# Ternary network: second products of even and odd tiles in two PSUM banks, the last two tiles in gate banks with scales of their own, and the last store in halves

## The chip, the cores and the metric

One core of a Trainium2 chip runs one program. The metric is the device time of that program in microseconds; three runs of the kernel before are shown.

## The reference

The program is a stack of four layers on x of shape 4 x 512 x 16 x 16 in f32 (1024 tokens of 512 channels): an attention layer, a mixture of experts, a scan over image rows, and last a feed-forward network with ternary weights. Only the last one is touched:

```python
    xn = _rmsnorm(x)                    # inside _bitlinear(x, w)
    scale = 127.0 / clip(max(abs(xn)), EPS);  xq = clip(round(xn * scale), -32, 127) / scale
    wq = clip(round(w / mean(abs(w))), -1, 1) * mean(abs(w))
    ...
    gate = silu(_bitlinear(x, w1))      # 512 -> 1408
    up = _bitlinear(x, w2)              # 512 -> 1408
    return _bitlinear(gate * up, w3)    # 1408 -> 512, then t = t + this
```

So h = gate * up needs its own mean square and its own maximum per token before it can be rounded and multiplied with w3. The maximum and the mean square run over all 1408 columns of a token.

## The kernel before

`ternary_ffn` is the last stage, from about 885 us on. The tokens stand in NT = 8 tiles of 128 (tile t is the tokens t * 128 and on). Each engine has a program of its own, written out by hand in the order in which it runs; semaphores with a running count tie them together. Per tile t:

- TensorE multiplies the rounded input `q_cm` with w1 and w2 in three parts (512, 512 and 384 columns). Part g = 3t + i goes to the gate banks `gu_ps[2 * (g % 2)]` (g0 or g1) and `gu_ps[2 * (g % 2) + 1]` (u0 or u1).
- ScalarE takes silu of the gate, VectorE multiplies by the other half into `h` (`h_ready`, a count of parts).
- VectorE takes the maximum (`h_max`), ScalarE the sum of squares (`square`, `hsq_ready`).
- VectorE works out the scales of a pair of tiles in a chain of small steps, each of which waits for the one before (`rsqrt`, `quant_scale`, L81 to L87 and L1920 to L1924; `hscale_ready`).
- ScalarE multiplies and rounds (`h_round`), VectorE clips to bf16 (`h_quant`, tile `hq`), TensorE transposes it into the banks `ht` (`turn_h`), ScalarE copies it to `h_cm` (`h_copy`).
- TensorE multiplies with w3 into the bank `y_ps` (`second`, 11 matmuls), VectorE adds to the tokens `x_tm` (`add_y`, `x4_ready`), TensorE transposes back into the bank `x_ps` (`turn_out`), ScalarE copies to `out_cm` (`out_copy`, `out_ready`), and SyncE stores one image (two tiles, 512 KB) at a time.

All eight PSUM banks are in use: g0, u0, g1, u1, two `ht`, `x_ps` and `y3_ps`. The pair (t - 3, t - 2) is finished while tile t (odd) is under way; the last pair, 6 and 7, comes after the loop. `second(t)` waits for `x4_ready` at t, because all tiles share `y_ps`; `turn_out(t)` waits for `out_ready` at t, because all share `x_ps`.

Of the kernel before, what the change touches and what calls it, by code (L numbers as in the profile page):

```python
# [1627 lines left out]
def ternary_ffn(nc, io, keep):  # L1628
# [7 lines left out]
    with ctx:  # L1636
# [72 lines left out]

        def col(i, t):  # L1710
            return stat[:, i, t:t + 1]
# [7 lines left out]

        def scale_and_round(eng, engine, t, done):  # L1720
            eng.wait_ge(q_scale_ready, t // HALF_TILES + 1)
            engine.tensor_scalar(z[:, t, :], z[:, t, :], col(Q, t), ROUND, ALU.mult, ALU.add).then_inc(done, 1)

        @block.sync
        def _(sp):
            for n in range(BATCH):
                sp.wait_ge(out_ready, 2 * n + 2)
                sp.dma_start(io["out"][n].rearrange("(k p) h w -> p k (h w)", p=P),
                             out_cm[:, :, n * SP:(n + 1) * SP]).then_inc(out_sent, 16)
            sp.wait_ge(out_sent, 16 * BATCH)  # L1730
# [11 lines left out]
        def _(act):  # L1742
# [24 lines left out]
            def h_round(t):  # L1767
                act.wait_ge(hscale_ready, t // 2 + 1)
                S.activation(h[:, t % 4, :], h[:, t % 4, :], ACT.Copy, bias=ROUND, scale=col(HQ, t)).then_inc(hr_ready, 1)
# [8 lines left out]
            def out_copy(t):  # L1778
                act.wait_ge(x4_turned, t + 1)
                S.copy(out_cm[:, :, t * P:(t + 1) * P], x_ps[:, :].rearrange("p (k m) -> p k m", k=KC)).then_inc(out_ready, 1)  # L1780
# [3 lines left out]
            for t in range(NT):  # L1784
                for i, (c, n) in enumerate(PARTS):
                    g = 3 * t + i
                    act.wait_ge(gu_summed, g + 1)
                    if g >= 2:
                        act.wait_ge(h_ready, g - 1)
                    S.activation(silu[:, g % 2, 0:n], gu_ps[2 * (g % 2)][:, 0:n], ACT.Silu,  # L1790
                                 scale=col(G_SCALE, t)).then_inc(silu_ready, 1)

                    if t % 2 == 0 and t >= 2 and i < 2:
                        h_round(t - 2 + i)
                    if t % 2 and t >= 3 and i == 0:
                        h_copy(t - 3)
                    if t % 2 and i == 1:
                        square(t - 1)
                for j in TURN_AFTER.get(t, ()):
                    q_copy(j)  # L1800
                if t >= 4 and t % 2 == 0:
                    out_copy(t - 4)
                if t % 2:
                    if t >= 3:
                        h_copy(t - 2)
                    square(t)
                    if t >= 5:
                        out_copy(t - 4)
            h_round(NT - 2)
            h_round(NT - 1)  # L1810
            out_copy(NT - 4)
            h_copy(NT - 2)
            out_copy(NT - 3)
            h_copy(NT - 1)
# [4 lines left out]
        def _(pe):  # L1819
# [30 lines left out]
            def second(t):  # L1850
                pe.wait_ge(h_cm_ready, 2 * t + 2)
                if t:
                    pe.wait_ge(x4_ready, t)
                else:
                    pe.wait_ge(x3_ready, NT)
                for k in range(W3):
                    mm = T.matmul(y_ps[:, :], h_cm[:, t % 2, k, :], w3[:, k, :], start=(k == 0), stop=(k == W3 - 1))  # L1857
                mm.then_inc(y_summed, 1)

            def turn_out(t):  # L1860
                pe.wait_ge(x4_ready, t + 1)
                if t:
                    pe.wait_ge(out_ready, t)
                for k in range(KC):
                    mm = T.transpose(x_ps[:, k * P:(k + 1) * P], x_tm[:, t, k * P:(k + 1) * P], ident[:, :])  # L1865
# [4 lines left out]
            for t in range(NT):  # L1870
# [14 lines left out]
                if t >= 4 and t % 2 == 0:  # L1885
                    turn_out(t - 4)
                if t % 2 and t >= 3:
                    turn_h(t - 2)
                    second(t - 3)
                    if t >= 5:  # L1890
                        turn_out(t - 4)
                    second(t - 2)
            turn_out(NT - 4)
            turn_h(NT - 2)
            turn_out(NT - 3)
            second(NT - 2)
            turn_h(NT - 1)
            second(NT - 1)
# [4 lines left out]
        def _(dve):  # L1903
# [56 lines left out]
            def add_y(t):  # L1960
                dve.wait_ge(y_summed, t + 1)
                V.scalar_tensor_tensor(x_tm[:, t, :], y_ps[:, :], col(Y_SCALE, t), x_tm[:, t, :],
# [25 lines left out]
            for t in range(NT):  # L1988
                for i, (c, n) in enumerate(PARTS):
                    g = 3 * t + i  # L1990
                    dve.wait_ge(silu_ready, g + 1)
                    V.scalar_tensor_tensor(h[:, t % 4, c:c + n], gu_ps[2 * (g % 2) + 1][:, 0:n], col(U_SCALE, t),  # L1992
                                           silu[:, g % 2, 0:n], ALU.mult, ALU.mult).then_inc(h_ready, 1)
# [6 lines left out]
                if t % 2:  # L2000
# [3 lines left out]
                    dve.wait_ge(dve_step, done[0])  # L2004
                    dve.wait_ge(hsq_ready, t + 1)
                    rsqrt(nc, link, cols(HRMS, t - 1, t + 1), cols(HSS, t - 1, t + 1), 1.0 / W1, RMS_EPS, scratch)
                    quant_scale(t - 1, t + 1, HRMS, HMAX, HA, HQ, Y_SCALE).then_inc(hscale_ready, 1)
                    link(V.tensor_scalar(cols(Y_SCALE, t - 1, t + 1), cols(Y_SCALE, t - 1, t + 1), inv_ws[:, 2:3], None, ALU.mult))
                    if t >= 3:
                        add_y(t - 2)  # L2010
            for t in (NT - 2, NT - 1):
                h_quant(t)
            for t in (NT - 2, NT - 1):
                add_y(t)
# [48 lines left out]
```

## Time and profile before

| | |
|---|---|
| median of 3 runs | 1003.87 us (999.87 to 1004.82) |
| profiled execution | 999.2 us, span 997.6 us |
| TensorE busy in the span | 929.6 us (93%) |
| VectorE, ScalarE busy | 634.0 us (64%), 543.4 us (54%) |
| mean granted clock of TensorE | 0.972 |

Positions in the text are microseconds from the span's start. The profiled time is that of the whole execution, the span what the profiler saw of it, first to last instruction or transfer. In the trace `h` is written at L1992, its maximum is L1952, `h_round` L1769, `square` L1765, `h_quant` L1958, `h_copy` L1775 and L1776, `second` L1857, `add_y` L1962, `turn_out` L1865, `out_copy` L1780 and the store L1728.

### The profile page before, as it was taken

How to read it: one execution, taken by the hardware profiler on the slowest of the kernel's cores; microseconds unless marked ns; L12 is line 12 of the kernel's file. 1: busy time of each engine (PE TensorE's matmuls, PEld its weight loads, DVE VectorE, ACT ScalarE, POOL GpSimd, SP SyncE). 2: the span in 40 equal slices, each digit the busy share in tenths (PEclk: the TensorE clock that was granted, in tenths of full speed). 3: DMA queues.
4: the chain of work that ended last, by engine and by line, in shares of the span. 5: the costliest groups of instructions: out<-in, count | busy, mean ns of one | idle time of the engine just before them, and what ended most of it. 6: DMA issues, size and time to landing. Idle time of an engine off the chain costs nothing. (4 is left out here: it accounts for less than half of the span.)

```text
span 997.6 us, 20461 instructions
## 1 busy us (share of the span) xinstructions
PE 929.6 (93%) x7568; PEld 612.2 (61%) x7569; DVE 634.0 (64%) x1281; ACT 543.4 (54%) x857; POOL 149.1 (15%) x174
## 2 busy tenths in 40 slices
PE   5998996999999999999999999999999979967795
PEld 4545543677766666766677677668764448743452
DVE  5388695557754645755656655665666876677673
ACT  3685776456654544655556655655653213235674
POOL 0000101001220120120120122012106720002000
PEclk9999998999999999999999999999999979987999
DMA  8770646678776567676578857857796610000001
GB/s 289 269 246 2 250 158 193 212 216 269 249 254 219 181 221 221 220 262 211 185 239 253 280 202 236 269 179 252 257 274 217 182 31 3 4 2 1 1 22 64
DMA packets 165038, 181.93 MB, mean 182 GB/s; under 512 B 54753, under 2 KB 132577, under 8 KB 164994
## 3 DMA queue, kind: packets, MB, share of 16 engines
q1 hardware_dynamic: 152354, 147.35, 45.8%
q0 software_dynamic: 9936, 32.12, 9.7%
q10 hardware_dynamic: 2704, 1.87, 0.6%
q8 instruction: 28, 0.46, 0.2%
q14 instruction: 16, 0.13, 0.0%
HBM read 155.09 MB, written 14.68 MB: 170 GB/s over the span
## 5 line engine op out<-in xcount | busy, mean ns | idle before, releaser
L1094 DVE SCALAR_TENSOR_TENSOR w_lo<-raw_first,w_hi 128x1024 f16<-128x1024 f32 x144 | 172.6, 1219 | 53.4 <-ACT w_hi L585 53.4
L852 PE MATMUL pa<-x,w_hi 128*128 128x256 f16 (+2 forms) x576 | 171.3, 297 | 2.9 <-DMA x<-early 2.5
L853 PE MATMUL pa<-x,w_hi 128*128 128x256 f16 (+2 forms) x576 | 171.3, 297 | 0.0
L854 PE MATMUL pa<-x,w_lo 128*128 128x256 f16 (+2 forms) x576 | 171.3, 297 | 0.0
L852 PE MATMUL pb<-x,w_hi 128*128 128x256 f16 (+2 forms) x576 | 170.6, 296 | 0.0
L853 PE MATMUL pb<-x,w_hi 128*128 128x256 f16 (+2 forms) x576 | 170.6, 296 | 0.0
L854 PE MATMUL pb<-x,w_lo 128*128 128x256 f16 (+2 forms) x576 | 170.6, 296 | 0.0
L1101 DVE SCALAR_TENSOR_TENSOR between<-pb,between 128x320 f32<-128x320 f32 (+1 forms) x144 | 73.8, 513 | 132.5 <-ACT between L589 132.4
L585 ACT ACTIVATE w_hi<-raw_first 128x1024 f16<-128x1024 f32 x144 | 147.8, 1050 | 15.3 <-PE pt L854 12.9
L1094 DVE SCALAR_TENSOR_TENSOR w_lo<-raw_last,w_hi 128x1024 f16<-128x1024 f32 x72 | 87.7, 1217 | 57.2 <-ACT w_hi L585 57.2
L593 ACT CAST early<-between 128x320 f16<-128x320 f32 (+1 forms) x144 | 68.4, 475 | 94.6 <-DVE between L1101 94.6
L585 ACT ACTIVATE w_hi<-raw_last 128x1024 f16<-128x1024 f32 x72 | 75.9, 1054 | 63.3 <-PE pe_ L926 27.2
L589 ACT ACTIVATE between<-pa 128x320 f32<-128x320 f32 (+1 forms) x144 | 65.3, 454 | 78.1 <-PE pb L854 77.5
L1106 DVE TENSOR_TENSOR early<-between,early 128x320 f16<-128x320 f32 (+1 forms) x144 | 73.1, 508 | 10.7 <-ACT early L593 10.5
L459 POOL DMA_DIRECT2D slot_y<-chunks x16 | 12.3, 767 | 416.5 <-ACT chunks L601 416.5
L852 PEld LDWEIGHTS pa<-x,w_hi 128*128 128x128 f16 x576 | 56.6, 98 | 25.0 <-issue 3.5
L854 PEld LDWEIGHTS pa<-x,w_lo 128*128 128x128 f16 x576 | 56.6, 98 | 20.4
L853 PEld LDWEIGHTS pa<-x,w_hi 128*128 128x128 f16 x576 | 56.5, 98 | 20.3
L852 PEld LDWEIGHTS pb<-x,w_hi 128*128 128x128 f16 x576 | 56.5, 98 | 20.0
L854 PEld LDWEIGHTS pb<-x,w_lo 128*128 128x128 f16 x576 | 56.4, 98 | 20.1
L853 PEld LDWEIGHTS pb<-x,w_hi 128*128 128x128 f16 x576 | 56.4, 98 | 19.9
L443 POOL DMA_INDIRECT early<-tokens,slot_ids x48 | 60.7, 1264 | 22.5 <-POOL slot_ids L451 12.8
(283 smaller groups left out, 1608.9 us busy)
## 6 DMA issues: line engine op xcount, KB each, us to landing
raw_first<-in_gate_up SPq DMA_DIRECT2D x96, 512.0 KB, 4.7
raw_last<-in_gate_up SPq DMA_DIRECT2D x32, 512.0 KB, 3.7
raw_first<-in_down SPq DMA_DIRECT2D x32, 512.0 KB, 5.0
raw_last<-in_down SPq DMA_DIRECT2D x32, 512.0 KB, 3.6
chunks<-in_f SPq DMA_DIRECT2D x16, 704.0 KB, 5.5
slot_y<-chunks POOLq DMA_DIRECT2D x16, 512.0 KB, 3.3
chunks<-in_f SPq DMA_DIRECT2D x6, 768.0 KB, 4.7
raw_first<-in_sgate SPq DMA_DIRECT2D x6, 512.0 KB, 6.0
```

Source lines behind the costliest of these rows:

```text
L443: pool.indirect_dma_start(out=rows16[0:w, j, :], out_offset=None, in_=io["tokens"], in_offset=bass.IndirectOffsetOnAxis(ap=ids[0:w, j:j + ...
L459: pool.dma_start(io["slot_y"][bass.ds(base_slot, 2 * P), :].rearrange("(j p) c -> p j c", p=P), y_sb[:, 0:2, :]).then_inc(y_out, 16)
L585: S.mul(w_hi[:, j % RING, c], raw[j % RING][:, c], W_SCALE).then_inc(hi_ready, 1)
L589: S.activation(gated[:, m % 2, 0:n], gate_ps[m % 2][:, 0:n], ACT.Silu, scale=1.0 / W_SCALE).then_inc(silu_ready, 1)
L593: S.copy(h_hi[:, m, 0:n], hid[:, m % 2, 0:n]).then_inc(h_hi_ready, 1)
L852: T.matmul(out, hi_a, hi_b, start=first, stop=False, **flags)
L853: T.matmul(out, hi_a, lo_b, start=False, stop=False, **flags)
L854: return T.matmul(out, lo_a, hi_b, start=False, stop=last, **flags)
L1094: V.scalar_tensor_tensor(w_lo[:, j % RING, c], raw[j % RING][:, c], W_SCALE, w_hi[:, j % RING, c], ALU.mult, ALU.subtract).then_inc(split_ ...
L1101: V.scalar_tensor_tensor(hid[:, m % 2, 0:n], up_ps[m % 2][:, 0:n], 1.0 / W_SCALE, gated[:, m % 2, 0:n], ALU.mult, ALU.mult).then_inc(hid_r ...
L1106: V.tensor_tensor(h_lo[:, m, 0:n], hid[:, m % 2, 0:n], h_hi[:, m, 0:n], ALU.subtract).then_inc(h_ready, 1)
```

## The change

Tiles share two banks in turn: `turn_ps(t)` is `x_ps` for even and `y_ps` for odd tiles, and both the second product of tile t and its transpose back use it. For tiles 6 and 7 the second product goes to g0 and g1, which the gates have left by then. `second(t)` waits for the output copy of tile t - 2 in place of the add of tile t - 1. Both transposes back of a pair and both output copies stand after the even tile's parts. For tile 7 the order is written out: tile 6 and tile 7 each get scales of their own (`SCALED` is the count of `hscale_ready` that a tile waits for), tile 6 is rounded, transposed and multiplied before tile 7's scales are ready, and the adds of tiles 4 and 5 come after tile 7's scales. The last image is stored in two halves, one for each tile. The other layers are unchanged.

```diff
@@ -1709,2 +1709,4 @@
+        SCALED = [1, 1, 2, 2, 3, 3, 4, 5]
+
         def col(i, t):
@@ -1719,2 +1721,8 @@
+        def turn_ps(t):
+            return (x_ps, y_ps)[t % 2]
+
+        def sum_ps(t):
+            return turn_ps(t) if t < NT - 2 else gu_ps[2 * (t - NT + 2)]
+
         def scale_and_round(eng, engine, t, done):
@@ -1725,3 +1733,3 @@
         def _(sp):
-            for n in range(BATCH):
+            for n in range(BATCH - 1):
                 sp.wait_ge(out_ready, 2 * n + 2)
@@ -1729,3 +1737,7 @@
                              out_cm[:, :, n * SP:(n + 1) * SP]).then_inc(out_sent, 16)
-            sp.wait_ge(out_sent, 16 * BATCH)
+            for t in range(NT - 2, NT):
+                sp.wait_ge(out_ready, t + 1)
+                sp.dma_start(io["out"][BATCH - 1].rearrange("(k p) h w -> p k (h w)", p=P)[:, :, t % 2 * P:(t % 2 + 1) * P],
+                             out_cm[:, :, t * P:(t + 1) * P]).then_inc(out_sent, 16)
+            sp.wait_ge(out_sent, 16 * (BATCH + 1))
@@ -1767,3 +1779,3 @@
             def h_round(t):
-                act.wait_ge(hscale_ready, t // 2 + 1)
+                act.wait_ge(hscale_ready, SCALED[t])
                 S.activation(h[:, t % 4, :], h[:, t % 4, :], ACT.Copy, bias=ROUND, scale=col(HQ, t)).then_inc(hr_ready, 1)
@@ -1779,3 +1791,3 @@
                 act.wait_ge(x4_turned, t + 1)
-                S.copy(out_cm[:, :, t * P:(t + 1) * P], x_ps[:, :].rearrange("p (k m) -> p k m", k=KC)).then_inc(out_ready, 1)
+                S.copy(out_cm[:, :, t * P:(t + 1) * P], turn_ps(t)[:, :].rearrange("p (k m) -> p k m", k=KC)).then_inc(out_ready, 1)
@@ -1794,5 +1806,7 @@
                         h_round(t - 2 + i)
+                    if t == NT - 1 and i == 0:
+                        square(t - 1)
                     if t % 2 and t >= 3 and i == 0:
                         h_copy(t - 3)
-                    if t % 2 and i == 1:
+                    if t % 2 and t < NT - 1 and i == 1:
                         square(t - 1)
@@ -1802,2 +1816,3 @@
                     out_copy(t - 4)
+                    out_copy(t - 3)
                 if t % 2:
@@ -1805,11 +1820,10 @@
                         h_copy(t - 2)
+                    if t == NT - 1:
+                        h_round(t - 1)
                     square(t)
-                    if t >= 5:
-                        out_copy(t - 4)
-            h_round(NT - 2)
+            h_copy(NT - 2)
             h_round(NT - 1)
+            h_copy(NT - 1)
             out_copy(NT - 4)
-            h_copy(NT - 2)
             out_copy(NT - 3)
-            h_copy(NT - 1)
             out_copy(NT - 2)
@@ -1851,8 +1865,10 @@
                 pe.wait_ge(h_cm_ready, 2 * t + 2)
-                if t:
-                    pe.wait_ge(x4_ready, t)
-                else:
+                if t < 2:
                     pe.wait_ge(x3_ready, NT)
+                elif t < NT - 2:
+                    pe.wait_ge(out_ready, t - 1)
+                else:
+                    pe.wait_ge(h_ready, 3 * (NT - 1) + t - NT + 4)
                 for k in range(W3):
-                    mm = T.matmul(y_ps[:, :], h_cm[:, t % 2, k, :], w3[:, k, :], start=(k == 0), stop=(k == W3 - 1))
+                    mm = T.matmul(sum_ps(t)[:, :], h_cm[:, t % 2, k, :], w3[:, k, :], start=(k == 0), stop=(k == W3 - 1))
                 mm.then_inc(y_summed, 1)
@@ -1861,6 +1877,6 @@
                 pe.wait_ge(x4_ready, t + 1)
-                if t:
-                    pe.wait_ge(out_ready, t)
+                if t >= NT - 2:
+                    pe.wait_ge(out_ready, t - 1)
                 for k in range(KC):
-                    mm = T.transpose(x_ps[:, k * P:(k + 1) * P], x_tm[:, t, k * P:(k + 1) * P], ident[:, :])
+                    mm = T.transpose(turn_ps(t)[:, k * P:(k + 1) * P], x_tm[:, t, k * P:(k + 1) * P], ident[:, :])
                 mm.then_inc(x4_turned, 1)
@@ -1886,2 +1902,3 @@
                     turn_out(t - 4)
+                    turn_out(t - 3)
                 if t % 2 and t >= 3:
@@ -1889,10 +1906,8 @@
                     second(t - 3)
-                    if t >= 5:
-                        turn_out(t - 4)
                     second(t - 2)
-            turn_out(NT - 4)
             turn_h(NT - 2)
-            turn_out(NT - 3)
             second(NT - 2)
             turn_h(NT - 1)
+            turn_out(NT - 4)
+            turn_out(NT - 3)
             second(NT - 1)
@@ -1961,3 +1976,3 @@
                 dve.wait_ge(y_summed, t + 1)
-                V.scalar_tensor_tensor(x_tm[:, t, :], y_ps[:, :], col(Y_SCALE, t), x_tm[:, t, :],
+                V.scalar_tensor_tensor(x_tm[:, t, :], sum_ps(t)[:, :], col(Y_SCALE, t), x_tm[:, t, :],
                                        ALU.mult, ALU.add).then_inc(x4_ready, 1)
@@ -1987,8 +2002,18 @@
             dve.wait_ge(dve_step, done[0])
-            for t in range(NT):
-                for i, (c, n) in enumerate(PARTS):
-                    g = 3 * t + i
-                    dve.wait_ge(silu_ready, g + 1)
-                    V.scalar_tensor_tensor(h[:, t % 4, c:c + n], gu_ps[2 * (g % 2) + 1][:, 0:n], col(U_SCALE, t),
-                                           silu[:, g % 2, 0:n], ALU.mult, ALU.mult).then_inc(h_ready, 1)
+            def gated(t, i):
+                g, (c, n) = 3 * t + i, PARTS[i]
+                dve.wait_ge(silu_ready, g + 1)
+                V.scalar_tensor_tensor(h[:, t % 4, c:c + n], gu_ps[2 * (g % 2) + 1][:, 0:n], col(U_SCALE, t),
+                                       silu[:, g % 2, 0:n], ALU.mult, ALU.mult).then_inc(h_ready, 1)
+
+            def h_scales(t0, t1):
+                dve.wait_ge(dve_step, done[0])
+                dve.wait_ge(hsq_ready, t1)
+                rsqrt(nc, link, cols(HRMS, t0, t1), cols(HSS, t0, t1), 1.0 / W1, RMS_EPS, scratch)
+                quant_scale(t0, t1, HRMS, HMAX, HA, HQ, Y_SCALE).then_inc(hscale_ready, 1)
+                link(V.tensor_scalar(cols(Y_SCALE, t0, t1), cols(Y_SCALE, t0, t1), inv_ws[:, 2:3], None, ALU.mult))
+
+            for t in range(NT - 1):
+                for i in range(len(PARTS)):
+                    gated(t, i)
                     if t % 2 == 0 and t >= 2 and i >= 1:
@@ -2003,13 +2028,20 @@
                         add_y(t - 3)
-                    dve.wait_ge(dve_step, done[0])
-                    dve.wait_ge(hsq_ready, t + 1)
-                    rsqrt(nc, link, cols(HRMS, t - 1, t + 1), cols(HSS, t - 1, t + 1), 1.0 / W1, RMS_EPS, scratch)
-                    quant_scale(t - 1, t + 1, HRMS, HMAX, HA, HQ, Y_SCALE).then_inc(hscale_ready, 1)
-                    link(V.tensor_scalar(cols(Y_SCALE, t - 1, t + 1), cols(Y_SCALE, t - 1, t + 1), inv_ws[:, 2:3], None, ALU.mult))
+                    h_scales(t - 1, t + 1)
                     if t >= 3:
                         add_y(t - 2)
-            for t in (NT - 2, NT - 1):
-                h_quant(t)
-            for t in (NT - 2, NT - 1):
-                add_y(t)
+
+            t = NT - 1
+            h_max(t - 1)
+            gated(t, 0)
+            h_scales(t - 1, t)
+            gated(t, 1)
+            gated(t, 2)
+            h_max(t)
+            h_quant(t - 1)
+            h_scales(t, t + 1)
+            add_y(t - 3)
+            add_y(t - 2)
+            h_quant(t)
+            add_y(t - 1)
+            add_y(t)
```

**TensorE, tiles 2 and 3 being finished** (at the end of tile 5; `ht` is the transposed h, `y_ps` and `x_ps` the two banks, `g` a gate bank). Before:

```order
L1847 MATMUL ht<-ident_b,hq 128x128 [waits h_cm_ready,hq_ready]
L1847 MATMUL ht<-ident_b,hq 128x128 x10
L1857 MATMUL y_ps<-ternary,h_cm 128x512 [waits x4_ready,h_cm_ready]
L1857 MATMUL y_ps<-ternary,h_cm 128x512 x10
L1865 MATMUL x_ps<-ident,x_tm 128x128 [waits out_ready,x4_ready]
L1865 MATMUL x_ps<-ident,x_tm 128x128 x3
L1857 MATMUL y_ps<-ternary,h_cm 128x512 [waits x4_ready,h_cm_ready]
L1857 MATMUL y_ps<-ternary,h_cm 128x512 x10
L1878 MATMUL g<-ternary,q_cm 128x512 [waits h3_ready,q_cm_ready]
L1878 MATMUL g<-ternary,q_cm 128x512 x3
```

Now:

```order
L1861 MATMUL ht<-ident_b,hq 128x128 [waits h_cm_ready,hq_ready]
L1861 MATMUL ht<-ident_b,hq 128x128 x10
L1873 MATMUL x_ps<-ternary,h_cm 128x512 [waits out_ready,h_cm_ready]
L1873 MATMUL x_ps<-ternary,h_cm 128x512 x10
L1873 MATMUL y_ps<-ternary,h_cm 128x512 [waits out_ready,h_cm_ready]
L1873 MATMUL y_ps<-ternary,h_cm 128x512 x10
L1894 MATMUL g<-ternary,q_cm 128x512 [waits h3_ready,q_cm_ready]
L1894 MATMUL g<-ternary,q_cm 128x512 x3
```

The second product of tile 3 follows that of tile 2 with no transpose between them and no wait for the add.

**TensorE, the end of the program,** from the second product of tile 5 on. Before:

```order
L1857 MATMUL y_ps<-ternary,h_cm 128x512 [waits x4_ready,h_cm_ready]
L1857 MATMUL y_ps<-ternary,h_cm 128x512 x10
L1865 MATMUL x_ps<-ident,x_tm 128x128 [waits out_ready,x4_ready]
L1865 MATMUL x_ps<-ident,x_tm 128x128 x3
L1847 MATMUL ht<-ident_b,hq 128x128 [waits h_cm_ready,hq_ready]
L1847 MATMUL ht<-ident_b,hq 128x128 x10
L1865 MATMUL x_ps<-ident,x_tm 128x128 [waits out_ready,x4_ready]
L1865 MATMUL x_ps<-ident,x_tm 128x128 x3
L1857 MATMUL y_ps<-ternary,h_cm 128x512 [waits x4_ready,h_cm_ready]
L1857 MATMUL y_ps<-ternary,h_cm 128x512 x10
L1847 MATMUL ht<-ident_b,hq 128x128 [waits h_cm_ready,hq_ready]
L1847 MATMUL ht<-ident_b,hq 128x128 x10
```

Now, from the same product:

```order
L1873 MATMUL y_ps<-ternary,h_cm 128x512 [waits out_ready,h_cm_ready]
L1873 MATMUL y_ps<-ternary,h_cm 128x512 x10
L1861 MATMUL ht<-ident_b,hq 128x128 [waits h_cm_ready,hq_ready]
L1861 MATMUL ht<-ident_b,hq 128x128 x10
L1873 MATMUL g<-ternary,h_cm 128x512 [waits h3_ready,h_cm_ready]
L1873 MATMUL g<-ternary,h_cm 128x512 x10
L1861 MATMUL ht<-ident_b,hq 128x128 [waits h_cm_ready,hq_ready]
L1861 MATMUL ht<-ident_b,hq 128x128 x10
L1881 MATMUL x_ps<-ident,x_tm 128x128 [waits x4_ready]
L1881 MATMUL x_ps<-ident,x_tm 128x128 x3
L1881 MATMUL y_ps<-ident,x_tm 128x128 [waits x4_ready]
L1881 MATMUL y_ps<-ident,x_tm 128x128 x3
```

Tile 6's transpose and second product (into `g`) follow tile 5's at once; the transposes back of tiles 4 and 5 stand between tile 7's transpose and its second product.

**VectorE, behind tile 7's scales** (`stat` holds the scales, L1924 and L1939 write the one that h is rounded by). Before:

```order
L1924 SCALAR_TENSOR_TENSOR stat<-stat 128x2 [waits dve_step3]
L2008 TENSOR_SCALAR stat<-stat,inv_ws 128x2
L1962 SCALAR_TENSOR_TENSOR x_tm<-y_ps,stat,x_tm 128x512 [waits y3_summed,dve_step3]
L1958 TENSOR_SCALAR hq<-h 128x1408 [waits h_turned,hr_ready] x2
L1962 SCALAR_TENSOR_TENSOR x_tm<-y_ps,stat,x_tm 128x512 [waits y3_summed] x2
```

Now:

```order
L1939 SCALAR_TENSOR_TENSOR stat<-stat 128x1 [waits dve_step3]
L2014 TENSOR_SCALAR stat<-stat,inv_ws 128x1
L1977 SCALAR_TENSOR_TENSOR x_tm<-x_ps,stat,x_tm 128x512 [waits y3_summed,dve_step3]
L1977 SCALAR_TENSOR_TENSOR x_tm<-y_ps,stat,x_tm 128x512 [waits y3_summed]
L1973 TENSOR_SCALAR hq<-h 128x1408 [waits h_turned,hr_ready]
L1977 SCALAR_TENSOR_TENSOR x_tm<-g,stat,x_tm 128x512 [waits y3_summed] x2
```

Before, both tiles were rounded after these scales; now tile 6's `hq` stands ahead of them, and two adds stand between the scales and tile 7's.

## Rows read from the trace of the kernel before

**Rows 1.** Busy us (instructions) per engine, granted clock, DMA, by windows.
```profile
...
960.00:970.00 10.00, 9.89 (x59) 5.10 (x58) 6.97 (x14) 7.04 (x10) 0.00 (x0) 1.00 0.04 11
...
```

**Rows 2.** Chain that ended last: start us, us, what.
```profile
...
983.23 3.85 PE y_ps L1857 x11
...
989.19 2.55 PE y_ps L1857 x11
...
993.61 0.58 ACT out_cm L1780
```

**Rows 3.** Timeline of the loop, TensorE: start, us, instruction, [idle before <-releaser].
```profile
...
940.04 2.53 PE L1857 MATMUL y_ps<-ternary,h_cm 128*128 128x512 fp8e4 x11 [1.37 <-DVE x_tm L1962]
...
956.24 0.60 PE L1865 MATMUL x_ps<-ident,x_tm 128*128 128x128 f32 x4
...
957.78 2.53 PE L1857 MATMUL y_ps<-ternary,h_cm 128*128 128x512 fp8e4 x11 [0.94 <-DVE x_tm L1962]
...
960.15 1.03 PE L1878 MATMUL g<-ternary,q_cm 128*128 128x512 fp8e4 x4
...
```

**Rows 4.** Timeline of tiles 6 and 7, ScalarE and VectorE.
```profile
...
962.08 0.69 ACT L1790 ACTIVATE silu<-g,stat 128x512 f32<-128x512 f32 x1 [4.28 <-PE u L1878]
...
967.09 0.88 DVE L1958 TENSOR_SCALAR hq<-h 128x1408 bf16<-128x1408 f32 x1
...
967.55 0.69 ACT L1790 ACTIVATE silu<-g,stat 128x512 f32<-128x512 f32 x1 [0.55 <-PE u L1878]
...
```

**Rows 5.** Groups by line and shape, 915 to 998: busy us, mean ns, idle before.
```profile
...
L1952 DVE TENSOR_REDUCE stat<-h 128x1 f32<-128x1408 f32 x8 | 12.9, 1613 | 0.1
L1769 ACT ACTIVATE h<-h,stat 128x1408 f32<-128x1408 f32 x8 | 11.6, 1461 | 6.2 <-DVE stat L1924 6.2
...
L1992 DVE SCALAR_TENSOR_TENSOR h<-u,stat,silu 128x512 f32<-128x512 f32 x14 | 10.5, 750 | 9.4 <-ACT silu L1790 9.2
...
L1958 DVE TENSOR_SCALAR hq<-h 128x1408 bf16<-128x1408 f32 x8 | 7.1, 886 | 1.1 <-ACT h L1769 1.1
...
L1992 DVE SCALAR_TENSOR_TENSOR h<-u,stat,silu 128x384 f32<-128x384 f32 x7 | 4.3, 618 | 4.7 <-ACT silu L1790 4.7
...
```

**Rows 6.** Timeline of VectorE, 974 to 998.
```profile
...
974.63 0.74 DVE L1962 SCALAR_TENSOR_TENSOR x_tm<-y_ps,stat,x_tm 128x512 f32<-128x512 f32 x1
975.29 0.16 DVE L81 TENSOR_SCALAR scratch<-stat 128x2 f32<-128x2 f32 x1
...
978.31 0.16 DVE L1924 SCALAR_TENSOR_TENSOR stat<-stat 128x2 f32<-128x2 f32 x1
...
978.65 0.75 DVE L1962 SCALAR_TENSOR_TENSOR x_tm<-y_ps,stat,x_tm 128x512 f32<-128x512 f32 x1
980.01 0.89 DVE L1958 TENSOR_SCALAR hq<-h 128x1408 bf16<-128x1408 f32 x1 [0.61 <-ACT h L1769]
...
991.78 0.75 DVE L1962 SCALAR_TENSOR_TENSOR x_tm<-y_ps,stat,x_tm 128x512 f32<-128x512 f32 x1 [3.90 <-PE y_ps L1857]
```

**Rows 7.** The last store: timeline, DMA queue and issue, window with rate.
```profile
994.22 0.37 SPq L1728 DMA_DIRECT2D out<-out_cm  x1
...
q10 hardware_dynamic: 2704, 1.87, 0.6%
...
out<-out_cm SPq DMA_DIRECT2D x1, 512.0 KB, 2.9
...
995.50:995.75 0.25, 0.00 (x0) 0.00 (x0) 0.00 (x0) 0.00 (x0) 0.00 (x0) 1.00 0.98 344
```

**Rows 8.** TensorE by windows: us, busy (x), granted clock, DMA.
```profile
893.00:894.00 1.00, 0.00 (x0) 0.88 0.00 0
...
910.00:911.00 1.00, 1.00 (x4) 0.59 0.00 0
...
982.50:983.00 0.50, 0.08 (x1) 0.50 0.00 0
...
985.50:986.00 0.50, 0.50 (x3) 0.58 0.98 346
```

More of the change, by code:

```diff
@@ L1851, in second @@
                 pe.wait_ge(h_cm_ready, 2 * t + 2)
-                if t:
-                    pe.wait_ge(x4_ready, t)
+                if t < 2:
+                    pe.wait_ge(x3_ready, NT)
+                elif t < NT - 2:
+                    pe.wait_ge(out_ready, t - 1)
                 else:
-                    pe.wait_ge(x3_ready, NT)
+                    pe.wait_ge(h_ready, 3 * (NT - 1) + t - NT + 4)
                 for k in range(W3):
-                    mm = T.matmul(y_ps[:, :], h_cm[:, t % 2, k, :], w3[:, k, :], start=(k == 0), stop=(k == W3 - 1))
+                    mm = T.matmul(sum_ps(t)[:, :], h_cm[:, t % 2, k, :], w3[:, k, :], start=(k == 0), stop=(k == W3 - 1))
                 mm.then_inc(y_summed, 1)
```

## The prediction

> **What bounds the kernel now.** The change touches only the last stage, which starts near 885 us of 997.6, so I read the stage by windows first, then the chain that ended last, then the timeline around the places the diff names. TensorE is busy for 9.89 us of 960 to 970 [rows 1]: the loop over tiles is close to full. The end is not. After tile 7's scales (their last step ends at 978.31 + 0.16 = 978.47 [rows 6]) the chain is one serial line: round, transpose, copy, and then two second products that start at 983.23 and 989.19, an output copy of 0.58 us at 993.61, and the store issued at 994.22 [rows 2, 7]. The span ends 3.4 us later. The second product of tile 6 also takes 3.85 us where tile 7's takes 2.55 [rows 2], at half the granted clock [rows 8].
>
> In the loop, the second products of tiles 1 and 3 wait 1.37 and 0.94 us for VectorE to have added the sum ahead, because both use y3_ps [rows 3]. That wait matters: ScalarE stands idle for 4.28 us until TensorE has tile 6's first gate [rows 4], and VectorE waits for ScalarE.
>
> **1. Two banks (and both output transposes after the even tile).** Tile 1's second product needs no add: it follows tile 0's directly, 1.37 us earlier by the wait and 0.17 more, as the end of a group runs over the start of the next (a group ends about 0.17 after the next can start: 957.78 + 2.53 against 960.15 [rows 3]). So tile 4 starts 1.54 us earlier. Its three parts stay that much ahead, but its two output transposes now stand ahead of tile 5 where one stood: one more costs TensorE 0.45 us (its row is 0.60, less the same overlap [rows 3]) and some slack there was hiding the first, so I count 0.56: tile 5 is 0.98 earlier. Then tile 3's second product saves the wait of 0.94 and the 0.60 of the transpose ahead of it [rows 3], 1.54: tile 6 starts 0.98 + 1.54 = 2.52 us earlier, at 957.6. Can VectorE and ScalarE follow? The preceding scales are ready 0.98 earlier, and VectorE's next add ends at 960.7, then the first gated part follows at 960.6 to 961.4, before TensorE wants its bank. ScalarE follows TensorE. So the rounded tile 5 on VectorE, which started at 967.09 and took 0.88 [rows 4], ends at 965.45, 2.52 earlier. Tile 7's first silu, after two transposes, comes 1.96 earlier: 967.55 becomes 965.6.
>
> What queues behind the new waits: a second product now waits for the output copy of two tiles before. For tile 4 that is tile 2's copy, which ScalarE makes after tile 6's third silu, near 964; the product starts near 969.7. It costs nothing, with 5 us of cover.
>
> **2. Scales of their own.** The chain of small steps is 3.36 us from its first step to the next instruction (975.29 to 978.65), 3.19 to the scale itself [rows 6], and one column instead of two saves nothing that I count. So VectorE gets one more chain, 3.36 us, and it lies on the path. Tile 7 on VectorE from 965.45: maximum of tile 6 1.61, gated part 0.75, scales of 6 3.36, gated parts 0.75 and 0.62, maximum 1.61, rounding of tile 6 0.89, chain to the scale 3.19 [rows 5, 6]: 12.78, less about 0.2 for neighbours that overlap by 0.08 (974.63 + 0.74 against 975.29 [rows 6]). Tile 7's scale is ready at 978.05, against 978.47: **0.4 us earlier only**. The 2.5 us from part 1 pay for the second chain. ScalarE keeps up, just: its square of tile 6 follows that first silu (965.6 + 0.69 [rows 4]) and, costed like its other pass over 1408 columns (1.46 [rows 5]), is ready at 967.75, when VectorE asks at 967.7.
>
> **3. Tile 6 off the tail.** This is where the gain is. With tile 6's scale at 970.9, ScalarE rounds it by 972.7, VectorE makes hq by 974.85, TensorE has done both pending second products by 974.5, transposes, and runs tile 6's second product at about 977.1 to 979.6, into g0: beside tile 7's scales instead of behind them. From tile 7's scale on, only its own line is left. Round 1.46 [rows 5]: 979.55. VectorE does the two delayed adds (0.75 each) from 978.2, until 979.65, so they cost at most 0.1. From the start of hq to the start of the second product: 983.23 - 980.01 = 3.22 [rows 2, 6]. Second product at 979.6 + 3.22 = 982.83, against 989.19: 6.36 earlier. The two output transposes ahead of it on TensorE (0.9) lie inside the wait for ScalarE's copy of the transposed h; the output copies of tiles 4 and 5 stand behind that copy and are done by 984, before tile 6's is wanted.
>
> **4. End.** Product to add 991.78 - 989.19 = 2.59 [rows 2, 6]: 985.42. Add, transpose and copy start: 0.75 + 0.06 + 0.67 = 1.48, since tile 7's transpose has a bank of its own (before, 993.61 - 991.78 = 1.83 [rows 2, 6]). The last copy ends at 987.5: 0.35 more. Gain so far 6.7.
>
> **5. Half a store.** Before, issue to landing 2.9 us for 512 KB, moved at 344 GB/s [rows 7], so 1.5 us of it is data. Half the bytes in as many packets, 512 B instead of 1 KB. At best half the data time goes, 0.77. At worst time goes by packets and nothing is saved. q10's packets, 692 B on average, took 0.6% of 16 engines' 997.6 us [rows 7]: 96 us over 2704, 35 ns, against 47 for 1 KB at 344 GB/s on 16 engines. I take 0.55, nearer to the byte end. The first half is issued 1 us earlier and has left the engines when the second starts. The Trainium skill, page DMA: Bandwidth & Descriptors, Specifications, gives 512 B as the smallest transfer at line rate; by that the half would save 0.77, and the whole sum would be 0.2 more. No row here has 512 B packets alone.
>
> **Sum.** 0.42 (scale) + 5.94 (tile 6 off the line; 1.3 of it is the slow clock) + 0.35 + 0.55 = 7.3 us. The profiled execution took 999.2 us (span 997.6 and 1.6 around it), so it becomes 991.9. It lay 4.7 below the median of the runs shown, 1003.87; against that the time is **996.6**.
>
> **Rivals.**
> *The clock falls in the new tail (20%).* TensorE now has idle stretches of some 1.5, 1.0 and 0.7 us between 975 and 983. Before, TensorE mostly waited after the loop, and the granted clock fell from full (2.4 GHz) to half near 982.5, until about 985.9 [rows 8]. The new tail is denser, which speaks against it. If it falls on tile 7's product: 3.85 - 2.55 = 1.3, up to 1.7 for half of those 3.4 us. Gain 5.6 to 6.0, 998.1. The Trainium skill, page TensorE: Matmul & The Clock Gate, section A second HAM failure mode, says that cycling through PSUM banks between groups of matmuls can make the clock swing; this change does cycle banks. That would be this rival; the trace before shows full clock in the loop [rows 1], where the gate banks already alternate.
>
> *The two-bank gain does not reach VectorE (15%).* Speaks for it: ScalarE and VectorE are 7 us busy of 10 [rows 1], and every handoff is tight. Then tile 7's VectorE work starts at 967.97 and all after it is 2.5 us later: gain 4.8, 999.1. No more than within 0.5%.
>
> *It does nothing (6%).* Some other wait, as for the rounded h or an instruction load, takes the tail back: 1003.9.
>
> *Slower, by a clock that stays half (4%).* Near 893.8 the granted clock fell to half and it came back only near 910.8, with TensorE fully busy by then [rows 8]. If the changed rhythm made it fall at tile 6, TensorE, full there, would lose half of the stretch. It decides from 14.6 us of half clock on; for 25 us, 12.5 - 7.3: 5 slower, 1009. Against it: the loop gets denser, not sparser.
>
> The forecast itself has 55%, with its own range of 995.7 to 998 from the store's ends and 0.7 of handoffs. The range for 8 in 10 takes in the first two rivals, and that the executions shown lie 5 us apart (999.87 to 1004.82): 992 to 1000.5. 0.5% is 5.0 us, about what a measurement here can tell from no change. Faster by more than that: the forecast, the clock rival and a part of the two-bank rival, less runs that scatter across the bound: 0.70. Within: 0.26. Slower: 0.04.
>
> **What would show it.** Step 1: no idle time before the second products of tiles 1, 3 and 5, tile 6's first gate near 957.6 and tile 7's first silu near 965.6. Step 2: two chains of 17 small steps on one column, VectorE busy without a break from 965 to 978, the last scale near 978.05. Step 3: tile 6's product into g0 before tile 7's scale is ready, 2.5 us long; the last product at 982.8. Step 4: last out_copy ends near 987.5. Step 5: landing below 2.9 us, near 2.35. Span near 990.3. Wrong if tile 6's h_copy makes ScalarE late for tile 7's rounding, if the last second product shows 0.43 us a matmul, or if the tile 7 scale is after 980.

## The result

| | before | this |
|---|---|---|
| median, 8 runs each | 999.75 us (998.17 to 1004.82) | 991.32 us (988.12 to 996.73) |
| profiled execution | 999.2 us, span 997.6 | 991.88 us, span 990.2 |

The ratio is 0.9903, 95% interval 0.9879 to 0.9928: 9.7 us faster, 7.2 to 12.1. It is not the quotient of the two medians, which lie 8.4 us apart. The prediction gave 996.6 us with a range from 992.0, so the time lies below the range. The gain was forecast at 7.3 us, at the lower end of the interval. The two profiled executions, the one of before being what the sum was made against, are 7.3 us apart (999.2 and 991.88), and the forecast of 991.9 for it is met. The agreement is closer than the sum deserves: the changed stretch, below, is 7.8 us shorter, and 0.4 us went the other way ahead of it.

To set the executions side by side I count from tile 0's second product, the first instruction that the change can reach: 936.13 before ([rows 3] show tile 1's, 3.91 us later), 936.53 after. From there to the end of the span it is 61.47 us before and 53.67 after. This is called the stretch below. It is 7.8 us shorter; all code ahead of it is the same in both.

The timeline of the changed kernel (start us, us, instruction, idle before it):

```profile
...
938.91 2.54 PE L1873 MATMUL y_ps<-ternary,h_cm 128*128 128x512 fp8e4 x11
...
955.59 2.54 PE L1873 MATMUL y_ps<-ternary,h_cm 128*128 128x512 fp8e4 x11
957.96 1.03 PE L1894 MATMUL g<-ternary,q_cm 128*128 128x512 fp8e4 x4
...
961.73 0.82 PE L1894 MATMUL g<-ternary,q_cm 128*128 128x384 fp8e4 x4 [0.15 <-DVE h L2006]
...
963.48 0.60 PE L1881 MATMUL y_ps<-ident,x_tm 128*128 128x128 f32 x4
...
965.71 1.61 DVE L1967 TENSOR_REDUCE stat<-h 128x1 f32<-128x1408 f32 x1
965.84 0.69 ACT L1802 ACTIVATE silu<-g,stat 128x512 f32<-128x512 f32 x1 [0.53 <-PE u L1894]
...
970.94 0.16 DVE L1939 SCALAR_TENSOR_TENSOR stat<-stat 128x1 f32<-128x1 f32 x1
...
972.33 2.54 PE L1873 MATMUL y_ps<-ternary,h_cm 128*128 128x512 fp8e4 x11
...
974.08 0.20 ACT L1777 ACTIVATION_READ_ACCUMULATOR hsq<-h 128x1 f32 x1
974.10 0.88 DVE L1973 TENSOR_SCALAR hq<-h 128x1408 bf16<-128x1408 f32 x1
...
977.32 2.55 PE L1873 MATMUL g<-ternary,h_cm 128*128 128x512 fp8e4 x11 [1.49 <-ACT h_cm L1788]
...
977.84 0.16 DVE L1939 SCALAR_TENSOR_TENSOR stat<-stat 128x1 f32<-128x1 f32 x1
...
979.54 0.89 DVE L1973 TENSOR_SCALAR hq<-h 128x1408 bf16<-128x1408 f32 x1
...
980.49 0.79 PE L1861 MATMUL ht<-ident_b,hq 128*128 128x128 bf16 x11 [0.63 <-DVE hq L1973]
...
982.76 2.55 PE L1873 MATMUL g<-ternary,h_cm 128*128 128x512 fp8e4 x11 [0.60 <-ACT h_cm L1788]
...
985.35 0.75 DVE L1977 SCALAR_TENSOR_TENSOR x_tm<-g,stat,x_tm 128x512 f32<-128x512 f32 x1 [4.26 <-PE g L1873]
...
986.85 0.59 ACT L1792 COPY out_cm<-y_ps 128x512 f32<-128x512 f32 x1 [0.48 <-PE y_ps L1881]
```

| from tile 0's second product, us | before | forecast | after |
|---|---|---|---|
| tile 6's first gate | 24.02 | 21.5 | 21.43 |
| tile 7's first silu | 31.42 | 29.5 | 29.31 |
| tile 7's scale done | 42.34 | 41.9 | 41.47 |
| tile 6's second product | 47.10 | 41.0 | 40.79 |
| tile 7's second product | 53.06 | 46.7 | 46.23 |
| last output copy done | 58.06 | 51.4 | 50.91 |
| end of the span | 61.47 | 54.2 | 53.67 |

Read it with the rows. The second products at 938.91 and 955.59 have no idle time in brackets, where [rows 3] have 1.37 and 0.94. Tile 6's product (977.32) starts before tile 7's scale (977.84) is written and lasts 2.55 us instead of 3.85 [rows 2]. Behind the scale the path has one round, one clip (979.54), one transpose (980.49), one copy and one product (982.76).

Busy time by windows (PE, PEld, DVE, ACT, POOL, then granted clock, DMA, GB/s):

```profile
960.00:970.00 10.00, 9.85 (x71) 5.70 (x70) 8.46 (x21) 9.47 (x14) 0.00 (x0) 1.00 0.15 53
970.00:980.00 10.00, 8.21 (x47) 3.63 (x44) 9.20 (x33) 7.14 (x9) 0.00 (x0) 1.00 0.01 2
```

In 960 to 970 VectorE is busy for 8.46 us and ScalarE for 9.47, against 6.97 and 7.04 before [rows 1]; in 970 to 980 VectorE is busy for 9.20. The granted clock of TensorE is 1.00 in both windows. The issues of the last two images' stores (what, count, KB, median us to landing), and a window in which the second half moves:

```profile
out<-out_cm SPq DMA_DIRECT2D x1, 512.0 KB, 2.9
out<-out_cm SPq DMA_DIRECT2D x2, 256.0 KB, 2.3
...
988.50:988.75 0.25, 0.00 (x0) 0.00 (x0) 0.00 (x0) 0.00 (x0) 0.00 (x0) 1.00 0.93 297
```

### The profile page after: what moved, and what is told of

The parts are those of the page before. It is cut to its first block and busy times, and to the rows that moved or that the text cites. A ratio compares the mean times of both kernels' runs of the same rounds, so it can differ in the third digit from the quotient of the medians.

```text
span 990.2 us, 20477 instructions
## 1 busy us (share of the span) xinstructions
PE 924.9 (93%) x7568; PEld 609.5 (62%) x7569; DVE 636.5 (64%) x1299; ACT 543.1 (55%) x857; POOL 149.4 (15%) x174
## 3 DMA queue, kind: packets, MB, share of 16 engines
q1 hardware_dynamic: 152882, 147.35, 46.7%
```

## Experiments

Each kernel from c_before on ran five rounds beside the kernel before; ratios are to that, each with its 95% interval. The stretch is from each one's profile, the span less the start of tile 0's second product; it is one execution of each kernel. "Slowest second product" is how long the slowest one took, 2.55 at full clock.

| run | stretch, us | slowest second product, us | ratio |
|---|---|---|---|
| before | 61.47 | 3.85 (tile 6) | |
| this | 53.67 | 2.55 | 0.9903 (0.9879 to 0.9928) |
| c_before | 61.00 | 3.06 (tile 6) | 1.0010 (0.9987 to 1.0032) |
| c_after | 53.73 | 2.55 | 0.9923 (0.9898 to 0.9947) |
| e1_banks | 59.65 | 3.91 (tile 6) | 0.9985 (0.9961 to 1.0009) |
| e2_tail_one_bank | 61.37 | 4.12 (tile 5) | 1.0004 (0.9974 to 1.0034) |
| e3_halves | 60.36 | 3.01 (tile 6) | 0.9982 (0.9966 to 0.9997) |
| e4_no_halves | 54.26 | 2.55 | 0.9924 (0.9897 to 0.9951) |
| e5_joint_scales | 59.54 | 4.79 (tile 6) | 0.9997 (0.9979 to 1.0016) |
| e6_short_chain6 | 53.21 | 2.55 | 0.9916 (0.9882 to 0.9949) |
| e7_warm_before | 60.17 | 2.55 | 0.9987 (0.9969 to 1.0005) |
| e8_split7 | 52.97 | 2.55 | 0.9918 (0.9900 to 0.9936) |
| e9_no_gate_banks | 56.74 | 4.18 (tile 7) | 0.9949 (0.9929 to 0.9968) |
| e10_split7_two_steps | 52.55 | 2.55 | 0.9912 (0.9889 to 0.9936) |

**Is the gain in the stretch, or elsewhere?** Both kernels again, unchanged.

> The kernel before, unchanged, against itself: how far apart two medians of one kernel come out. If the part of the measured gain beyond what the tail shows is scatter of the executions, the ratio is 1 with an interval of some 0.3% either way, and the stretch from tile 0's second product to the span's end is 61.5 us as in the first profile, whatever the span is. If the last stage itself varies from one execution to the next (a clock that falls or not), this stretch moves by 1 us or more.

> The changed kernel again. Theory 1 (all of the gain lies behind tile 0's second product, the rest is scatter): that stretch is 53.7 us again, 7.8 less than before, and the ratio is near 0.992. Theory 2 (the change also makes the layers ahead faster, by its place in memory or its instruction loads): the ratio is again 0.990, and the position of tile 0's second product lies 1 to 2 us earlier than in the kernel before.

The kernel before, in the timeline of TensorE:

```profile
...
935.90 2.54 PE L1857 MATMUL y_ps<-ternary,h_cm 128*128 128x512 fp8e4 x11
...
980.76 1.14 PE L1847 MATMUL ht<-ident_b,hq 128*128 128x128 bf16 x11 [2.48 <-DVE hq L1958]
...
983.38 3.06 PE L1857 MATMUL y_ps<-ternary,h_cm 128*128 128x512 fp8e4 x11 [0.55 <-ACT h_cm L1776]
...
988.54 2.55 PE L1857 MATMUL y_ps<-ternary,h_cm 128*128 128x512 fp8e4 x11 [1.49 <-ACT h_cm L1776]
```

and the changed one:

```profile
...
936.17 2.54 PE L1873 MATMUL x_ps<-ternary,h_cm 128*128 128x512 fp8e4 x11
...
982.41 2.55 PE L1873 MATMUL g<-ternary,h_cm 128*128 128x512 fp8e4 x11 [0.61 <-ACT h_cm L1788]
```

The stretch is 53.73 us again, to 0.06, and the ratio 0.9923 puts the gain at 7.7 us (5.3 to 10.2). Theory 1 fits: 7.3 to 7.8 us lie behind tile 0's second product, and the ratio asks for no more. The kernel before is not as steady: 61.00 for 61.47, with tile 6's product at 3.06 instead of 3.85 us, so its last stage does vary, by the clock. Theory 2 had tile 0's product 1 to 2 us earlier in the changed kernel. It starts at 935.90 and 936.17 here, 936.13 and 936.53 in the first pair: not earlier in either, though two pairs are weak evidence beside the scatter below.

What moves the time of a single execution most is the part ahead. Over all fourteen profiles, with one code for it, tile 0's product starts between 934.25 (e10_split7_two_steps) and 941.94 (e3_halves), 7.7 us apart. The medians of the kernel before were 1003.87 (the 3 runs shown), 999.75 (8), 1001.61 (12, c_before), 1000.69 (35), 999.36 (23) and 999.67 (18); the 8 include the 3.

**The two banks alone.**

```diff
 # before, with turn_ps(t) = (x_ps, y_ps)[t % 2] in second, add_y, turn_out, out_copy
-                if t:
-                    pe.wait_ge(x4_ready, t)
+                if t < 2:
+                    pe.wait_ge(x3_ready, NT)
                 else:
-                    pe.wait_ge(x3_ready, NT)
+                    pe.wait_ge(out_ready, t - 1)
...
                     turn_out(t - 4)
+                    turn_out(t - 3)
 # likewise out_copy(t - 3); turn_out no longer waits for out_ready
```

> The two banks and the moved output transposes alone; joint scales, the old tail and a whole store. By my sum tile 7's first silu comes 2.0 us earlier and, with no second chain of small steps on VectorE, so does everything after it: stretch 59.5 us, ratio 0.998. Rival (VectorE or ScalarE bounds the loop): under 0.5 us.

```profile
...
934.45 2.54 PE L1859 MATMUL x_ps<-ternary,h_cm 128*128 128x512 fp8e4 x11
...
977.18 1.35 PE L1849 MATMUL ht<-ident_b,hq 128*128 128x128 bf16 x11 [4.02 <-DVE hq L1957]
...
980.02 3.91 PE L1859 MATMUL x_ps<-ternary,h_cm 128*128 128x512 fp8e4 x11 [0.63 <-ACT h_cm L1779]
...
986.03 2.55 PE L1859 MATMUL y_ps<-ternary,h_cm 128*128 128x512 fp8e4 x11 [1.49 <-ACT h_cm L1779]
```

The stretch is 59.65 us, 1.8 less; I expected 59.5. Its ratio can't be told from 1. The work itself comes earlier than that: ScalarE starts to round tile 6 at 974.72, 2.11 us earlier in the stretch than before (978.51). Some 0.3 us of it is lost again to the clock, which had fallen ahead of tile 6's transposes here: they took 1.35 us, against 0.79 in the first profile of the kernel before, and the product 3.91 against 3.85.

**The new tail without the two banks.**

```diff
 # after, with y_ps for second(0) to second(5) and x_ps for all output transposes
+            add_y(t - 3)
             h_scales(t, t + 1)
-            add_y(t - 3)
             add_y(t - 2)
```

> The rewritten tail, own scales, gate banks and the halved store, but one bank for all products up to tile 5 and one for all output transposes; the add of tile 4 has to stand ahead of tile 7's scales. My sum: tile 7's VectorE line starts 2.5 us later than in the changed kernel, tile 5's product waits for the add of tile 4, tile 6's copy then delays tile 7's rounding: last second product near 4.6 us later than in the changed kernel, stretch 58.5 us. If the two parts were independent it would be 7.8 - 2.0 = 5.8 faster than before, 55.7.

```profile
...
978.77 4.12 PE L1874 MATMUL y_ps<-ternary,h_cm 128*128 128x512 fp8e4 x11 [2.76 <-DVE x_tm L1979]
...
985.00 2.55 PE L1874 MATMUL g<-ternary,h_cm 128*128 128x512 fp8e4 x11 [1.49 <-ACT h_cm L1788]
...
990.23 0.63 PE L1882 MATMUL x_ps<-ident,x_tm 128*128 128x128 f32 x4 [1.62 <-ACT out_cm L1792]
990.69 2.54 PE L1874 MATMUL g<-ternary,h_cm 128*128 128x512 fp8e4 x11
```

It is 61.37 us: nothing gained, where I expected 58.5. Tile 5's product waits 2.76 us for the add of tile 4, and after that idle time it runs at half clock, 4.12 us. The wait was in my sum, the clock was not: 1.6 us (4.12 against 2.53). Nor was a second wait: the output transposes of tiles 4 and 5 share one bank, TensorE waits 1.62 us for a copy between them, and tile 7's product starts at 990.69, 1.1 us after its input was copied (989.60). So the last product comes 7.4 us later in the stretch than in the changed kernel, where I expected 4.6. The parts are far from independent: the new tail needs the second bank, since otherwise tile 5's product, and tile 6 behind it, wait for an add that VectorE reaches late.

**Own scales.**

```diff
 # after, with one h_scales(6, 8) behind h_max(7), square(6) and h_round(6) at their old places
-            h_scales(t - 1, t)
...
-            h_scales(t, t + 1)
+            h_scales(t - 1, t + 1)
```

> The changed kernel with one chain of scales for tiles 6 and 7 together, so that tile 6 is rounded and multiplied behind it; two banks, gate banks and halved store stay. By my sum the scales are ready 1.5 us earlier than in the changed kernel but both products lie behind them: the stretch from tile 0's second product to the end is 57.2 us with the clock at full, 58.5 if it falls on tile 6's product as in the kernel before. That would give own scales 3.5 to 4.8 of the 7.8 us. If they gave nothing it would be 53.7.

```profile
...
981.15 1.09 PE L1858 MATMUL ht<-ident_b,hq 128*128 128x128 bf16 x11 [4.33 <-DVE hq L1970]
983.73 4.79 PE L1870 MATMUL g<-ternary,h_cm 128*128 128x512 fp8e4 x11 [1.49 <-ACT h_cm L1788]
...
990.62 2.55 PE L1870 MATMUL g<-ternary,h_cm 128*128 128x512 fp8e4 x11 [0.60 <-ACT h_cm L1788]
```

The stretch is 59.54 us, above both values expected, because the clock costs more than I had allowed: 4.79 - 2.55 = 2.24 on the product and 0.3 on the transposes (1.09 against 0.79). Without it the stretch would be 57.0 to 57.3, where I expected 57.2. Own scales give 3.3 to 3.6 us of the gain by order, and keep TensorE from the wait of 4.33 us ahead of tile 6's transpose, after which the clock is at half for almost the whole product.

**The gate banks.**

```diff
-            return turn_ps(t) if t < NT - 2 else gu_ps[2 * (t - NT + 2)]
+            return turn_ps(t)
 # second(6) and second(7) wait for out_ready at 5 and 6; turn_out(4) and turn_out(5) ahead of
 # second(6), out_copy(4) and out_copy(5) ahead of h_round(7)
...
-            h_scales(t, t + 1)
             add_y(t - 3)
             add_y(t - 2)
+            h_scales(t, t + 1)
```

> The changed kernel with the second products of tiles 6 and 7 in the two shared banks instead of the gate banks. The adds of tiles 4 and 5 must then stand ahead of tile 7's chain of scales on VectorE, which is busy without a break there: two adds of 0.75 us less their overlap, 1.4 us, put tile 7's scale and all behind it that much later: stretch from tile 0's second product to the end 55.1 us against 53.7. If gate banks gave nothing it is 53.7; if tile 6's product, now behind two output copies, holds up tile 7, it is over 56.

```profile
...
978.53 2.53 PE L1871 MATMUL x_ps<-ternary,h_cm 128*128 128x512 fp8e4 x11 [0.88 <-ACT out_cm L1792]
...
984.77 4.18 PE L1871 MATMUL y_ps<-ternary,h_cm 128*128 128x512 fp8e4 x11 [1.49 <-ACT h_cm L1788]
```

Tile 7's product starts 984.77 - 937.16 = 47.61 us into the stretch, 1.38 later than in the changed kernel (46.23), as expected. It then takes 4.18 us, mostly at half clock, 1.63 more, which I had not expected here. The stretch, 56.74, lies where I had put "over 56", but not for the reason given there: tile 6's product is only 0.6 us later (first row, behind an output copy), and what goes beyond 55.1 is the clock. So the clock rival is real; it stands close by the changed kernel.

**Is the clock's fall due to idle time?** In the first profile of the kernel before, TensorE waits 2.47 us ahead of tile 6's transposes:

```profile
980.96 0.79 PE L1847 MATMUL ht<-ident_b,hq 128*128 128x128 bf16 x11 [2.47 <-DVE hq L1958]
```

Needless matmuls fill this wait:

```diff
             turn_out(NT - 4)
+            pe.wait_ge(h_ready, 3 * NT)
+            for k in range(11):
+                T.matmul(gu_ps[0][:, :], h_cm[:, 1, k, :], w3[:, k, :], start=(k == 0), stop=(k == 10))
             turn_h(NT - 2)
```

> The kernel before with 11 needless matmuls of 512 columns on TensorE, into a gate bank that nobody reads again, in the gap between tile 4's output transpose and tile 6's transpose (2.5 us idle). If the idle time made the clock fall on tile 6's second product, that one takes 2.5 us instead of 3.85 and the stretch is 60.2 us instead of 61.5. If the fall has another cause, nothing or some 0.2 us more.

```profile
...
980.93 2.54 PE L1896 MATMUL g<-ternary,h_cm 128*128 128x512 fp8e4 x11
...
985.84 2.55 PE L1857 MATMUL y_ps<-ternary,h_cm 128*128 128x512 fp8e4 x11 [0.66 <-ACT h_cm L1776]
```

The needless matmuls (980.93) keep the granted clock up, tile 6's product takes 2.55 us, and the stretch is 60.17: 1.3 less than 61.47, 0.8 less than 61.00. So the idle time was the cause, as far as one profile shows it, and 0.8 to 1.3 us of the 7.3 to 7.8 is the clock.

**The half store.**

```diff
-            for n in range(BATCH):
+            for n in range(BATCH - 1):
...
+            for t in range(NT - 2, NT):        # and the reverse, on the changed kernel
+                sp.wait_ge(out_ready, t + 1)
...
```

> The kernel before with only the last store in halves: 0.6 us less in the stretch by its landing time (60.9 from 61.5, give or take what the clock does to tile 6's product), not to be told from 1 in the ratio. In this tail the two output copies are 1.4 us apart, so the first half has left before the second is issued.

> The changed kernel with the last image stored whole. Stretch 0.6 us longer (landing 2.9 for 2.3), ratio to the changed kernel not to be told from 1.

The stretch is 0.59 longer without halves (54.26 against 53.67), and 60.36 with halves alone, against 61.00 in the profile whose tile 6 product is as long (3.06 and 3.01). The last image lands 2.9 us after its issue when whole, its halves 2.3 us after theirs. 0.6 us, as summed.

**What bounds tile 7 in the new order?**

```diff
-            h_scales(t - 1, t)
+            h_scales(t - 1, t, 1)
 # the last argument: rounds of the refinement, 3 elsewhere
```

> The changed kernel with one step of refinement instead of three in tile 6's inverse root: six small VectorE instructions less, about 1.2 us (it changes tile 6's scale in its last digits). If VectorE bounds tile 7 without a break, tile 7's scale and the end come 1.2 us earlier; if ScalarE or TensorE does, under 0.3.

```profile
...
976.16 1.38 ACT L1777 ACTIVATE hsq<-h 128x1408 f32<-128x1408 f32 x1
...
977.73 0.15 DVE L81 TENSOR_SCALAR scratch<-stat 128x1 f32<-128x1 f32 x1 [0.53 <-ACT hsq L1777]
```

Only 0.46 to 0.52 us of the 1.2 came through. VectorE now waits 0.53 us for ScalarE's square of tile 7, which stands behind tile 6's rounding. So VectorE bounds this piece, but ScalarE is only half a microsecond behind.

**Further along the same line.**

```diff
-            h_round(NT - 1)
+            for a, b in ((0, 1024), (1024, W1)):
+                S.activation(h[:, t % 4, a:b], h[:, t % 4, a:b], ACT.Copy, bias=ROUND, scale=col(HQ, t)).then_inc(hr_ready, 1)
 # likewise h_quant(7), turn_h(7), h_copy(7) and second(7); turn_out(4) ahead of turn_h(7)
```

> The changed kernel with tile 7's rounding, clipping, transposing and copying in two pieces (columns 0 to 1023 and the rest), so that VectorE, TensorE and ScalarE overlap on what is now a serial line of 4.7 us from the scale to the second product. The copy of the first piece can start some 0.9 us earlier and the product needs only that piece to start: last product 1.3 us earlier, stretch 52.4 us. If fixed costs of the smaller pieces eat it: 53.5.

```profile
...
977.06 1.65 ACT L1828 ACTIVATE h<-h,stat 128x1024 f32<-128x1024 f32 x2 [0.78 <-DVE stat L1958]
...
979.86 1.01 ACT L1831 COPY h_cm<-ht 128x1024 bf16<-128x1024 bf16 x1 [1.14 <-PE ht L1924]
...
981.01 2.53 PE L1931 MATMUL g<-ternary,h_cm 128*128 128x512 fp8e4 x11 [0.37 <-ACT h_cm L1831]
```

> The same with two steps of refinement instead of three in the inverse roots of tiles 6 and 7 (a relative error of some 5e-6 in their scales): three small VectorE instructions less in each chain, 0.58 us. Tile 7's chain lies bare, so its 0.58 is sure; tile 6's counts only as far as ScalarE's square of tile 7 is early, 0.5 by the run with one step: stretch 51.3 us, ratio to the kernel before 0.990.

```profile
...
974.69 2.55 PE L1880 MATMUL g<-ternary,h_cm 128*128 128x512 fp8e4 x11 [1.49 <-ACT h_cm L1788]
...
975.92 0.96 DVE L2065 TENSOR_SCALAR hq<-h 128x1024 bf16<-128x1024 f32 x2 [0.38 <-ACT h L1828]
...
977.08 0.60 PE L1888 MATMUL x_ps<-ident,x_tm 128*128 128x128 f32 x4
...
977.52 0.78 PE L1924 MATMUL ht<-ident_b,hq 128*128 128x128 bf16 x11
```

The first saves 0.70 us (1.3 expected), the second 0.42 more (1.1 expected). The last rows show the reason for the second: VectorE has the first piece ready near 976.6 (an estimate: both pieces are in one row, 0.96 us from 975.92), but TensorE is on tile 6's product until 977.08, and an output transpose stands next, so the transposes of tile 7 start at 977.52. There TensorE has become the wait. Both give the shortest stretches of all; their ratios (0.9918, 0.9912) can't be told from that of the changed kernel.

## Why the prediction was wrong, and where it was right

**The step that failed** is the last one of the sum: "It lay 4.7 below the median of the runs shown, 1003.87; against that the time is 996.6". The median of three runs was taken as the kernel's time. It was 2.3 to 4.5 us high: the other five medians of the same kernel lie between 999.36 and 1001.61. Of the 5.3 us between 996.6 and 991.32, 4.1 are this base (1003.87 against 999.75) and 1.1 the gain (8.4 between the medians against 7.3). The forecast gain of 7.3 on 999.75 would have been 992.5. The scatter sits ahead of tile 0's second product, where the same code takes 934 to 942 us. The range named the 5 us between executions, but did not let the base itself be 4 us lower. The mechanism was right, and the terms of the sum held, as follows.

**Two banks**: right. 1.96 forecast for tile 7's first silu, 2.1 seen; with the banks alone (e1_banks) 2.1 at tile 6's rounding and 1.8 at the end. Two small terms were loose. The second output transpose was counted as 0.56 us though the rows gave 0.45; it cost 0.47 (tile 4 starts 1.53 earlier, tile 5 1.06). And VectorE was said to be ready before TensorE wants its bank; in tile 6 TensorE waits 0.15 us for it (961.73).

**Scales of their own**: right in kind. "0.4 us earlier only" for tile 7's scale; it was 0.87: the row of VectorE's work starts 0.14 us earlier than forecast (965.71), and it is 0.3 shorter, since a chain took 3.10 us to its scale rather than 3.19 and the neighbours overlap more than the 0.2 that I took off. Nearly all of the 0.5 us by which the stretch beats the forecast is this.

**Tile 6 off the tail**: right, 41.0 forecast and 40.79 seen for its product, 46.7 and 46.23 for tile 7's. That it is the main gain follows from e5_joint_scales: without it 5.9 us of the 7.8 are gone, 2.2 to 2.5 of them by the clock.

**End and half store**: right. From tile 7's product to the last copy's end it is 4.68 us instead of 5.00, 0.32 saved where 0.35 was forecast. The landing fell from 2.9 to 2.3 us where I took 0.55. In 512 B pieces the second half moved at 287 to 297 GB/s, in 1 KB pieces the whole image at 344 [rows 7]; at 290 the half takes 0.90 us where the image took 1.52, 0.6 less by this estimate. By the Trainium skill's rule (DMA: Bandwidth & Descriptors, Specifications) that 512 B is enough for line rate it would have been 0.77, by my estimate; the trace lies between that and a cost by packets.

**The rivals.** The clock did not fall in the six profiles that have the changed tail's order. With one more wait in it (e9_no_gate_banks) it did, at 1.63 us, within the price named. The falls follow waits on TensorE: 2.47 and 2.48 us in the kernel before, 4.02 in e1_banks, 4.33 in e5_joint_scales, 2.76 in e2_tail_one_bank, three of 0.88, 1.44 and 1.49 in e9_no_gate_banks. The Trainium skill (TensorE: Matmul & The Clock Gate, A second HAM failure mode) ties a swinging clock to cycling through PSUM banks, with short idle stretches of TensorE between groups of matmuls. Here cycling by itself did not bring it: the changed kernel and e5_joint_scales write to the same banks, and only the second, with its wait of 4.33 us, fell. That VectorE or ScalarE would not follow the banks is refuted by e1_banks. That the change does nothing is refuted by both ratios. Slower by a clock that stays half was not seen.

**The excess of the first ratio** (9.7 us against 7.8 in the stretch) is not explained by any row. Its interval, 7.2 to 12.1, holds the 7.8, the medians lie 8.4 apart, and the second ratio gives 7.7. For every other variant too, what its stretch gains on 61.2 (between the two profiles of the kernel before) lies within the interval of its ratio. So it can be scatter; what makes the part ahead vary was not tried.

## What to carry to other kernels

A second chain of small steps on a busy engine can pay, if it lets a neighbour's long work leave the serial line at the end; but it needs the slack that another edit makes (here the second bank): without that bank the whole new tail gave nothing. Lay the last tile out as a list of each engine's work with durations from the trace: that gave every position within 0.6 us. Don't anchor a time on a median of three when single executions lie 0.5% apart (over 35 of them, 996.3 to 1007.78, it is 1.1%); forecast the difference, and let the range carry the base's own doubt.

## What was not expected of the hardware

In every profile of the old tail TensorE waited before tile 6's transpose, and the granted clock was at half when tile 6's product began; but the price differed from one execution of the same code to the next: tile 6's product took 3.85 and 3.06 us. In the first the clock fell near 982.5, behind the transposes, and was back near 985.9; in the second it fell within them (granted 0.64 in 980.9 to 981.4) and was back by 984.5. There the transposes took 1.14 us instead of 0.79, and less of the product ran slow. At half clock for almost all of it, the product took 4.79 against 2.55 (e5_joint_scales). Eleven needless matmuls in the gap won 0.8 to 1.3 us (e7_warm_before).
